# Moving the middle of three maximum steps behind both score tiles in a two-layer decoder kernel

## The reference, cut to what matters

```
q = (x @ Wq).reshape(B, Nq, HEADS, DIM_HEAD)          # 8 heads of 64, 1024 queries
k = (context @ Wk).reshape(B, context.shape[1], HEADS, DIM_HEAD)
v = (context @ Wv).reshape(B, context.shape[1], HEADS, DIM_HEAD)
sim = jnp.einsum('bihd,bjhd->bhij', q, k) * SCALE
attn = jax.nn.softmax(sim, axis=-1)
out = jnp.einsum('bhij,bjhd->bihd', attn, v)
```

## Time and profile before

| | |
|---|---|
| median of 3 runs | 1639.53 us (1639.24 to 1639.96) |
| the profiled execution, its own time | 1638.51 us |
| its span, first to last instruction | 1636.8 us |
| mean granted TensorE clock | 0.964 |
| layer 0's cross attention in the span | 128.6 to 1003 us |

### The profile page before, as it was taken

The page is one execution under the profiler, slowest core; times in us unless marked ns, Lnnn a source line. Parts: engine busy times, 40 slices in busy tenths (PEclk is TensorE's granted clock), DMA queues, the critical chain, the costliest instruction groups (busy, mean ns, idle before and its releaser), DMA issues.

```text
span 1636.8 us, 27033 instructions
## 1 busy us (share of the span) xinstructions
PE 1530.1 (93%) x9058; PEld 548.9 (34%) x9058; DVE 1286.3 (79%) x2319; ACT 1126.0 (69%) x1541; POOL 490.9 (30%) x488
## 2 busy tenths in 40 slices
PE   6889999999999999999999998899997979999986
PEld 4312333333333333333333223344444612222223
DVE  6898987879977779878789897877775666787766
ACT  6787777768877778777777786655554469676643
POOL 6303343334543334433300010345451012233100
PEclk9759999999999999999999998999999979999998
DMA  4000000000200000000010000111100000000000
GB/s 135 7 1 11 1 1 1 1 2 11 54 1 2 1 1 1 3 1 11 20 32 3 1 1 19 37 46 45 45 27 1 1 1 2 0 1 1 1 14 13
DMA packets 14834, 22.79 MB, mean 14 GB/s; under 512 B 1990, under 2 KB 11766, under 8 KB 14710
## 3 DMA queue, kind: packets, MB, share of 16 engines
q1 hardware_dynamic: 14710, 21.22, 4.6%
HBM read 20.69 MB, written 0.52 MB: 13 GB/s over the span
## 4 chain that ended last, share of the span: by engine, by line
PE 69%; issue 11%; DVE 9%; POOL 5%; ACT 4%; DMA 0%; POOLq 0%; SPq 0%; DVEq 0%; ACTq 0%
PE PS L2167 22%; PE PS L2153 15%; PE PS L2511 6%; PE PS L2199 5%; POOL WRK L734 5%; PE PS L2498 3%; DVE KNB L1382 3%; PE PS L2020 2%; PE PS L2012 2%; PE PS L2116 2%; PE PS L2540 2%; PE PS L2450 1%; PE PS L2435 1%; PE PS L2004 1%; ACT KNB L959 1%
## 5 line engine op out<-in xcount | busy, mean ns | idle before, releaser
L1382 DVE CUSTOM_DVE_ANT_0 KNB<-PS,KNB 128x512 f16<-128x512 f32 (+2 forms) x500 | 338.5, 690 | 152.4 <-PE PS L2199 106.9
L1432 DVE TENSOR_TENSOR WRK<-WRK 128x768 f32<-128x768 f32 (+3 forms) x400 | 425.2, 1063 | 15.3 <-ACT WRK L933 8.4
L933 ACT ACTIVATE WRK<-PS 128x1024 f32<-128x1024 f32 (+1 forms) x408 | 401.4, 1022 | 47.6 <-PE PS L2153 39.2
L2167 PE MATMUL PS<-WRK,V 128*64 128x512 f32 (+1 forms) x1632 | 395.7, 605 | 0.0
L708 POOL TENSOR_TENSOR WRK<-WRK 128x256 f32<-128x256 f32 x300 | 274.7, 916 | 395.6 <-ACT WRK L933 394.6
L959 ACT ACTIVATE KNB<-PS 128x512 f16<-128x512 f32 (+2 forms) x306 | 180.9, 591 | 77.8 <-PE PS L2199 77.2
L2344 PE MATMUL PS<-WRK,KNB 128*128 128x512 f16 x828 | 188.3, 381 | 7.1 <-POOL WRK L734 2.7
L2167 PEld LDWEIGHTS PS<-WRK,V 128*64 128x64 f32 (+1 forms) x1632 | 99.3, 136 | 192.7 <-issue 154.5
L2153 PE MATMUL PS<-KNB,KB 64*128 64x512 f16 (+1 forms) x1224 | 156.5, 377 | 0.0
L2153 PE MATMUL PS<-Q,KB 64*128 64x512 f16 (+1 forms) x1224 | 153.0, 377 | 0.0
L1162 ACT ACTIVATE WRK<-PS 128x1024 f32<-128x1024 f32 x100 | 102.4, 1024 | 51.1 <-PE PS L2498 47.6
(11 more groups left out here) (379 smaller groups left out, 1834.2 us busy)
## 6 DMA issues: line engine op xcount, KB each, us to landing
V<-in_moe_w_dram SPq DMA_DIRECT2D x44, 192.0 KB, 2.4
KNB<-in_ctx_fm_dram SPq DMA_DIRECT2D x6, 384.0 KB, 8.4
X<-in_ctx_fm_dram SPq DMA_DIRECT2D x12, 192.0 KB, 2.4
CTX<-in_ctx_fm_dram SPq DMA_DIRECT2D x6, 384.0 KB, 3.9
BW<-in_bit_w_dram SPq DMA_DIRECT2D x1, 960.0 KB, 9.8
PWK<-in_pair_w_dram SPq DMA_DIRECT2D x4, 192.0 KB, 2.8
XT<-in_x_fm_dram SPq DMA_DIRECT2D x1, 512.0 KB, 5.0
X<-in_x_tm_dram SPq DMA_DIRECT2D x1, 512.0 KB, 12.0
```

Of the source, the lines that this page charges most:

```text
L933: e.activation(PR[0:r, u % 2, b, :], bank(2 * b, 2 * b + 2, slice(0, r)), ACT.Exp).then_inc(S("exp"), 1)
L1382: return e.tensor_tensor_reduce(diffs, sums, diffs, 0.5, NEG, ALU.add, ALU.max, accum_out=out)
L1432: e.tensor_tensor(total, total, part, ALU.add).then_inc(S("acc"), 1)
L2167: ins = e.matmul(PS[h * HD:(h + 1) * HD, 4, :], V[0:r, j, h * HD:(h + 1) * HD], PR[0:r, unit_no(hf, i) % 2, b, h * HALF:(h + 1) * HALF], s ...
```

## The change

In a slot with three steps, PE issues the middle step after the scores of both tiles and ahead of the value block; before, it stood between the two tiles' scores. ACT takes the middle step's absolute value after both exponentials; before, between them. The last step has a second place in the code, between the two tiles of `values`, for a slot with a middle step and no value block.

```diff
@@ ACT, the loop over pairs and slots @@
                     magnitude(p, first)
                     exp(hf, i, 0)
-                    magnitude(p, mid)
                     for x in filter(inside, ITEMS[p][s]):
                         bank5(x)
                     if len(tiles_of(i)) > 1:
                         exp(hf, i, 1)
+                    magnitude(p, mid)
                     magnitude(p, last)
@@ PE, the same loop @@
                     max_steps(p, first)
                     scores(hf, i, 0)
-                    max_steps(p, mid)
                     for x in filter(inside, ITEMS[p][s]):
                         bank5(x)
                     if len(tiles_of(i)) > 1:
                         scores(hf, i, 1)
+
+                    max_steps(p, mid)
+                    makes_values = any(x[0] == "v" for x in ITEMS[p][s])
                     for x in ITEMS[p][s]:
                         if x[0] == "v" and mid:
                             bank5(x)
-                    max_steps(p, last)
+                    if makes_values or not mid:
+                        max_steps(p, last)
...
                         for b in tiles_of(before[1]):
                             values(*before, b)
+                            if b == 0 and mid and not makes_values:
+                                max_steps(p, last)
```

## The result

| kernel | median | lowest to highest | runs |
|---|---|---|---|
| before | 1639.47 us | 1639.24 to 1643.72 | 6 |
| changed | 1647.04 us | 1646.16 to 1650.92 | 6 |

The ratio is 1.0046, with a 95% interval of 1.0032 to 1.0059: slower by 7.6 us, between 5.2 and 9.7 by the interval. The forecast was 1646.4, 6.9 more than before.

A forecast was written before the change was run, and what follows sets the result against it. PE (TensorE) was taken to bound the kernel, busy 93% of the span and 859.68 of 874.40 us in layer 0's cross attention. Terms 5.1 + 0.2 + 1.5 = 6.9 us on 1639.5 gave 1646.4, range 1644.0 to 1650.5.

The forecast's parts named there:

- The middle step's wait on DVE goes: PE, three-step slots: middle step starts at +1.51 without its 0.42 us wait; slot 44 still held by DVE to +1.79.
- The new wait on ACT: Last step waits for the absolute value behind both exponentials, starting at +3.61 (slot 48: +3.50); net +0.57 us in 9 slots.
- What PE loses by it: On PE, the value block ends at +2.51 and PE stands for 1.10 us until the last step at +3.61.
- The sum: Over all 15 slots: 5.1 + 0.2 + 1.5 = 6.9 us slower, nothing taken off for PE's other idle time.
- The dead hunk: Last step's second place, between the two tiles of values: claimed to issue nothing in any slot.
- Faster: Rival, at ACT: the new wait is nil and only the gain is left, 7.8 us, 1631.7; chance 3%.
- Nothing took up the delay: Rival of no change: a wait further on takes up the delay, leaving under 0.2% (3.3 us); chance 4%.
- DVE did not get late: Rival of slower by much more: DVE or the value copy gets late, 15 x 1.10 = 16.5 us, 1656; chance 7%.
- The clock in the stretch stayed at 1.00: Rival: PE's clock falls to 1.2 GHz behind each new stall, 72 us more, 1718; chance 1%.

The follow-up runs named there:

- pe_only: Changed kernel with ACT's middle absolute value put back between the two exponentials, PE's order as changed; 1635.80 us, ratio to before 0.9981.
- last_between: Changed kernel with the last step of the 15 slots issued on PE between the two tiles of values; 1635.82 us, ratio to before 0.9975.
- no_third_hunk: Changed kernel without the last step's second place in the code and the variable makes_values; 1646.20 us, ratio to before 1.0041.
- last_between_pe: last_between with ACT's order as before the change, middle absolute value between the exponentials; 1635.63 us, ratio to before 0.9979.

## Why the prediction was right

Forecast 1646.4 in a range of 1644.0 to 1650.5, measured 1647.04. Step by step:

- *The middle step's wait on DVE goes.* Predicted start +1.51, measured 285.99 - 284.48 = +1.51. (In slot 48 it is +1.47.) The list of waits fell from 7.1 to 1.9 us on DVE; I had written 4. In slot 44 the step is still late (+1.78) and still held by DVE, whose read ends at 325.67 and which releases the step at 325.81. But the twelve score matmuls now fill the time up to 325.71 by their modelled end, so the bracket names nobody, and the 2 us that I left to DVE there are not in the list.
- *The new wait on ACT.* Predicted +3.61 for slots 36 and 44 and +3.50 for slot 48; measured +3.61, +3.61 and +3.51. The price was read from slot 26, where the same order of two exponentials and an absolute value already stood in the trace, and it carried over to 0.01 us. In the list, L2199 on ACT rose by 15 entries and 13.0 us (12 predicted). pe_only shows by intervention that the place on ACT makes the loss, and last_between that it costs only because no runnable work stands ahead of the wait in PE's queue.
- *What PE loses by it.* I had the value block end at +2.51 and PE stand for 1.10 us. It ends at +2.61: from the middle step to the value block are 0.32 us, not 0.22, so the 0.1 of a hand-over was not regained and PE stands for 1.00. ACT sets the last step's start either way, and the sum does not use this term.
- *The sum.* 6.9 predicted (the terms as they stand add up to 6.8), 6.9 by the slots, 7.6 between the medians with an interval that holds both. The 0.7 in between is not the slots'; no_third_hunk, with the same slots, lies at 6.6. The cause of the 0.7 stays open; the profiled executions of before and changed differ by 5.4 us outside of the maximum steps, some 3 of them in two parts where the clock differs. PE's idle time in the stretch grew by 8.4 us where I had written 7, with the roughness of these totals named above.
- *The dead hunk* was dead (no_third_hunk).
- *The rivals.* Faster did not come, but its size was instructive: last_between takes the wait away by covering it and gains 4.8 us, where I had priced 7.8 for the case of no new wait at all. Of the 3.0 us between these two figures, 15 x 0.15 = 2.2 is the split of `values`, and 3 x 0.27 = 0.8 is slot 44, whose middle step remains held by DVE (+1.78 in each variant with the moved step). The 7.8 had counted that wait as gone, against the prediction's own working for slot 44. Nothing took up the delay. DVE did not get late: its middle maximum was over 0.94 us ahead of the last step. The clock in the stretch stayed at 1.00 although PE stood still, by the brackets, for 0.93 us in nine of the slots, 0.87 in three and 0.66 in three.
- TensorE: Matmul & The Clock Gate, section "HAM oscillation", in the Trainium skill warns of idle gaps that throttle the clock. Stalls of up to 0.93 us, spaced by 20 us, did not throttle it here. The waits in the section's example are several times as long, so the trace does not speak against it.

## What to carry to other kernels

Reordering one engine's queue to take its wait away is half of an edit; the engine that releases the next wait has a queue as well, and moving both in parallel can be worse than moving one. Here the same move gained 3.8 us on PE alone, and lost 7.6 with its mirror on ACT. Before pricing a new order, look in the trace for a place where it already happens by chance, and when a wait can't be shortened, put runnable work in front of it.

## What the runs showed of the hardware

A group of eight fp32 `values` matmul records cut in two by a pair of fp16 matmuls of another kind took 1.01 to 1.02 us for each half up to the next work, against 1.87 for the whole, some 0.15 us for the cut (last_between, last_between_pe, changed). I had expected the halves to be free. In the executions profiled here, a part of layer 1 with the same instructions was 1.7 us longer at the lower granted clock (63.15 us at 0.90 against 64.85 at 0.86), and the whole spans of two programs with the same instructions differed by 4.4 us (1644.8 and 1649.2), more than half of what was to be measured; the slot lengths, in a stretch with a clock of 1.00, repeated to 0.02.
